# Last mixture's combine: rows read place by place behind a data-dependent gate, all adding on VectorE

## The reference, cut to what matters

```python
w, sel = _route(x, gate_weight, expert_bias)          # 4 distinct experts of 16 per token
cw = (one_hot(sel, NUM_EXPERTS) * w[..., None]).sum(1)
def body(acc, inp):
    g, u, d, we = inp
    y = silu(x @ g.T) * (x @ u.T) @ d.T
    return (acc + we[:, None] * y, None)
out, _ = lax.scan(body, zeros_like(x), (gate_proj, up_proj, down_proj, cw.T))
...
x = x + tanh(g_ffn[3]) * (out + shared)
```

## Time and profile before

| | us |
|---|---|
| median of 3 runs | 1233.58 |
| the profiled execution's own time | 1233.05 |
| its span, first to last instruction | 1231.3 |
| last tile's scatter starts on POOL | 1194.59 |
| first read of the combine issued | 1197.97 |
| DVE's 64 additions | 1201.25 to 1227.69 |

### The profile page before, as it was taken

The page is one execution under the profiler, slowest core; times in us unless marked ns, Lnnn a source line. Parts: engine busy times, 40 slices in busy tenths (PEclk is TensorE's granted clock), DMA queues, the critical chain, the costliest instruction groups (busy, mean ns, idle before and its releaser), DMA issues. The chain is left out here.

```text
span 1231.3 us, 25490 instructions
## 1 busy us (share of the span) xinstructions
PE 1056.1 (86%) x7158; PEld 776.4 (63%) x7159; DVE 747.1 (61%) x2777; ACT 497.3 (40%) x1341; POOL 605.1 (49%) x945
## 2 busy tenths in 40 slices
PE   4988799999999998699998989948886958799970
PEld 4556688886777775356556778725554536588850
DVE  6766545234444443789975565566778776555548
ACT  0056321213333332378772234415664633244430
POOL 5652006762333334666662535535655766455550
PEclk9988799999999998699998999957999978899995
DMA  9889922223333333422520245340001622466648
GB/s 399 243 321 399 405 111 85 103 95 88 108 104 108 108 104 114 139 95 87 215 70 28 80 136 154 118 146 1 2 2 49 242 80 98 129 165 163 165 123 325
DMA packets 71646, 175.75 MB, mean 143 GB/s; under 512 B 11438, under 2 KB 38318, under 8 KB 70446
## 3 DMA queue, kind: packets, MB, share of 16 engines
q1 hardware_dynamic: 50297, 117.84, 29.3%
q0 software_dynamic: 17664, 48.91, 10.9%
q10 hardware_dynamic: 3600, 7.95, 1.7%
HBM read 85.89 MB, written 88.76 MB: 142 GB/s over the span
## 5 line engine op out<-in xcount | busy, mean ns | idle before, releaser
L2349 PE MATMUL bank<-weights,xT 128*128 x832 | 240.6, 412 | 0.2 <-ACT xT L2445 0.2
L2168 POOL DMA_INDIRECT slots_out<-weights,y_rows x128 | 122.7, 959 | 114.5 <-DVE y_rows L2616 67.1
L2162 POOL DMA_INDIRECT slots_in<-xn_wide,row_in x110 | 106.7, 970 | 118.2 <-ACT rows L2421 58.7
L2349 PEld LDWEIGHTS bank<-weights,xT 128*128 128x128 f32 x832 | 142.4, 191 | 24.6 <-issue 0.7
L2168 POOL DMA_INDIRECT slots_out<-pack,y_rows x80 | 76.7, 959 | 137.0 <-DVE y_rows L2616 112.4
L2445 ACT COPY xT<-bank 128x256 f32<-128x256 f32 x208 | 77.5, 373 | 115.1 <-PE bank L2341 114.9
L2258 PE MATMUL bank<-xT,weights 128*128 128x256 f32 x416 | 105.1, 398 | 2.3 <-ACT xT L2409 2.3
L1574 PE MATMUL bank<-ctx,weights 32*128 32x256 f32 x512 | 77.8, 449 | 31.0 <-DVE weights L1730 25.3
L1647 ACT ACTIVATE weights<-bank 128x512 f32<-128x512 f32 x128 | 72.6, 596 | 57.9 <-PE bank L1582 57.9
L1730 DVE TENSOR_REDUCE weights<-bank 128x2 f32<-128x512 f32 x128 | 85.6, 682 | 15.3 <-PE bank L1574 15.0
L2593 DVE TENSOR_TENSOR weights<-weights,bank 128x128 f32<-128x128 f32 x128 | 36.8, 288 | 93.3 <-ACT weights L2449 93.2
(11 more groups left out here) (436 smaller groups left out, 2435.4 us busy)
## 6 DMA issues: line engine op xcount, KB each, us to landing
slots_in<-gbias SPq DMA_DIRECT2D x11, 3072.0 KB, 25.6
weights<-slots_in SPq DMA_DIRECT2D x96, 132.0 KB, 2.3
xs_wide<-slots_in SPq DMA_DIRECT2D x72, 132.0 KB, 2.2
weights<-slots_out SPq DMA_DIRECT2D x17, 512.0 KB, 9.6
rows<-slots_out SPq DMA_DIRECT2D x16, 512.0 KB, 3.5
weights<-in_l_gu SPq DMA_DIRECT2D x1, 7040.0 KB
pack<-slots_in SPq DMA_DIRECT2D x40, 132.0 KB, 2.1
weights<-in_l_gu SPq DMA_DIRECT2D x1, 4352.0 KB, 13.7
```

Source lines behind the costliest of these rows:

```text
L2162: pool.indirect_dma_start(out=slots_in, in_=xn_wide[:, t, :], in_offset=None, out_offset=bass.IndirectOffsetOnAxis(ap=row_in[:, t, i:i + 1 ...
L2168: pool.indirect_dma_start(out=slots_out, in_=y[:, n % U, :], in_offset=None, out_offset=bass.IndirectOffsetOnAxis(ap=y_rows[:, n % U:n % U ...
L2349: last = nc.tensor.matmul(out, xT[:, n.c % 2, c, :], flat(gu_w[:, ds(e, 1), c, :]), start=(c == 0), stop=(c == C - 1 and layer != 2))
```

## The change

`combine_last()` goes. Its work moves to the end of the queues inside `mixture(3, ...)`:

- DVE works out in `rank_experts`, for the experts 12, 13, 14 and 15, how many turns of 8 tiles the tiles up to that expert take, times 16, into `turns_past` (four more small instructions).
- SP, when it has issued the last tile's load, does four times, for the places 3, 2, 1, 0: it reads a number of `turns_past` into a register, waits until all eight `stored[u]` have reached it, and issues the read. Places 3, 2 and 1 are one DMA of 2 MB each, into `ctx`, `ctxT` and `xn`, which nothing needs any more; place 0 is four DMAs of 512 KB (4 blocks each) into the space of the first 8 experts' weights. All pieces are now 1 KB.
- DVE goes from the loop straight into the same 64 additions, in pairs of blocks, places 3, 2, 1, 0 within a pair. An addition of place 3, 2 or 1 waits for that place's whole DMA, one of place 0 for the quarter that its block is in.
- The output stores are issued by SP, behind the reads.

The diff also has code for PE, ACT and POOL to take a part of the adding. It is not used: `TURNED` and `POOLED` are empty.

```diff
@@ rank_experts
+        if layer == 3:
+            turns = routed // 8
+            begun = rt["go_on"][:, 0:4 * turns].rearrange("p (e j) -> p e j", j=turns)
+            need = rt["go_on"][:, 4 * turns:4 * turns + 4]
+            step(nc.vector.tensor_scalar(need, cum[:, NE - 4:NE], 1.0 / 8, None, ALU.mult))
+            step(nc.vector.tensor_tensor(begun, need.unsqueeze(2).broadcast_to([P, 4, turns]),
+                                         numbers[:, 0:turns].unsqueeze(1).broadcast_to([P, 4, turns]), ALU.is_gt))
+            step(nc.vector.tensor_reduce(need, begun, AX.X, ALU.add))
+            step(nc.vector.tensor_scalar(turns_past[:], need, 16.0, None, ALU.mult))
+            yield
@@ mixture
+            if layer == 3:
+                row_home = (weights[:, 0:NB * D].rearrange("p (t d) -> p t d", t=NB), xn,
+                            ctxT[:].rearrange("p t c q -> p t (c q)"), ctx[:])
+                of_token = slots_out[0:NB * P * 4].rearrange("(t p i) d -> p t i d", p=P, i=4)
...
+                OWN = tuple(("rows", t, t + 1) for t in range(0, NB, 2))
+                TURNED, POOLED = (), ()
+                STORES = tuple((t, t + 2) for t in range(0, NB, 2))
...
+                def wait_row(eng, t, i):
+                    if i:
+                        eng.wait_ge(early_in[i], 16)
+                    else:
+                        eng.wait_ge(last_in[t // 4], 16)
@@ sync
+                if layer == 3:
+                    for i in (3, 2, 1, 0):
+                        past = sp.value_load(turns_past[0:1, 3 - i:4 - i], min_val=32, max_val=16 * (total // U))
+                        for u in range(U):
+                            sp.wait_ge(stored[u], past)
+                        if i:
+                            sp.dma_start(row_home[i], of_token[:, :, i, :]).then_inc(early_in[i], 16)
+                        else:
+                            for q in range(4):
+                                few = slice(4 * q, 4 * q + 4)
+                                sp.dma_start(row_home[0][:, few], of_token[:, few, 0, :]).then_inc(last_in[q], 16)
+                    for t0_, t1_ in STORES:
...
+                            sp.wait_ge(added, finished[t1_ - 1])
+                        sp.dma_start(io["out"][:, t0_:t1_, :], x[:, t0_:t1_, :]).then_inc(out_stored, 16)
+                    for u in range(U):
+                        sp.wait_ge(stored[u], total // U * 16)
+                    sp.wait_ge(out_stored, 16 * len(STORES))
@@ vector
-                for i in range(U):
-                    dve.wait_ge(stored[i], total // U * 16)
+                if layer < 3:
+                    for i in range(U):
+                        dve.wait_ge(stored[i], total // U * 16)
+                    return
...
+                    for i in (3, 2, 1, 0):
+                        for t in of:
+                            wait_row(dve, t, i)
+                            if i < 3:
+                                dve.wait_ge(added, done + 1 - len(of))
+                            nc.vector.scalar_tensor_tensor(x[:, t, :], row_home[i][:, t, :], weight[:, t, i:i + 1],
                                                            x[:, t, :], ALU.mult, ALU.add).then_inc(added, 1)
+                            done += 1
@@ the block that goes
-    def combine_last():
...
-                for t in range(NB):
-                    sp.dma_start(rows[:, t], of_token[:, t]).then_inc(ready[t], 16)
...
-                for t in range(0, NB, 2):
-                    act.wait_ge(added, place(t + 1, n - 1))
-                    act.dma_start(io["out"][:, t:t + 2, :], x[:, t:t + 2, :]).then_inc(out_stored, 16)
...
-                for pair in range(0, NB, 2):
-                    for i in range(n):
-                        for t in (pair, pair + 1):
```

More of the change, by code:

```diff
@@ L170, in _build @@
     tile_block = sb("tile_block", [1, ROUTED], I32)
+    turns_past = sb("turns_past", [P, 4], I32)
     lanes = sb("lanes", [P, 4])
@@ L2082, in mixture @@
                 gb = gbias[:].rearrange("p (e n) -> p e n", e=NE)
+            if layer == 3:
+                row_home = (weights[:, 0:NB * D].rearrange("p (t d) -> p t d", t=NB), xn,
+                            ctxT[:].rearrange("p t c q -> p t (c q)"), ctx[:])
+                of_token = slots_out[0:NB * P * 4].rearrange("(t p i) d -> p t i d", p=P, i=4)
+                last_in = [sem(f"last_in{i}") for i in range(4)]
+                early_in = [None] + [sem(f"early_in{i}") for i in range(1, 4)]
+                added, diag_ready, mixed, scaled, pooled = (
+                    sem(n) for n in ("added", "diag", "mixed", "scaled", "pooled"))
+                diag = row_space[:, 0:8 * P].rearrange("p (u i q) -> p u i q", u=2, i=4)
+                turned_banks = [bank[i] for i in (0, 1, 2, 3, 6, 7)]
+                OWN = tuple(("rows", t, t + 1) for t in range(0, NB, 2))
+                TURNED, POOLED = (), ()
+                STORES = tuple((t, t + 2) for t in range(0, NB, 2))
+                finished, done = {}, 0
+                for kind, *of in OWN:
+                    done += 4 * len(of) if kind == "rows" else len(of)
+                    for at, t in enumerate(of):
+                        finished[t] = done - (len(of) - 1 - at)
+                def wait_row(eng, t, i):
[3 more added lines that the diff above has]
+                        eng.wait_ge(last_in[t // 4], 16)
             E_I = m["E_I"]
@@ L2170, in _ @@
                                             ).then_inc(stored[n % U], 16)
+                if layer == 3 and POOLED:
+                    pool.wait_ge(sh_added, NB)
+                    for at, t in enumerate(POOLED):
+                        for i in (3, 2, 1, 0):
+                            pool.wait_ge(scaled, 4 * at + 4 - i)
+                            if i < 3:
+                                pool.wait_ge(pooled, 4 * at + 3 - i)
+                            nc.gpsimd.tensor_tensor(x[:, t, :], x[:, t, :], row_home[i][:, t, :], ALU.add
+                                                    ).then_inc(pooled, 1)
             @block.sync
@@ L2381, in _ @@
                 each_step(pe, step)
+                if layer == 3:
+                    for q, t in enumerate(TURNED):
+                        for i in (3, 2, 1, 0):
+                            wait_row(pe, t, i)
+                            pe.wait_ge(diag_ready, 4 * q + 4 - i)
+                            last = nc.tensor.matmul(turned_banks[q][:, 0:D], diag[:, q % 2, i, :], row_home[i][:, t, :],
+                                                    start=(i == 3), stop=(i == 0))
+                        last.then_inc(mixed, 1)
             @block.scalar
@@ L2460, in _, with weigh_ident, weigh @@
                 each_step(act, step)
+                def weigh_ident(q):
+                    if q >= 2:
+                        act.wait_ge(mixed, q - 1)
+                    for i in (3, 2, 1, 0):
+                        nc.scalar.activation(diag[:, q % 2, i, :], ident[:], ACT.Copy,
+                                             scale=weight[:, TURNED[q], i:i + 1]).then_inc(diag_ready, 1)
+                def weigh(t):
+                    for i in (3, 2, 1, 0):
+                        wait_row(act, t, i)
+                        nc.scalar.activation(row_home[i][:, t, :], row_home[i][:, t, :], ACT.Copy,
+                                             scale=weight[:, t, i:i + 1]).then_inc(scaled, 1)
+                if layer == 3 and TURNED:
+                    weigh_ident(0)
+                    weigh_ident(1)
+                    for at in range(3):
+                        weigh(POOLED[at])
+                        weigh_ident(2 + at)
+                    weigh_ident(5)
             @block.vector
@@ L2623, in _ @@
                 each_step(dve, tile_step)
-                for i in range(U):
-                    dve.wait_ge(stored[i], total // U * 16)
-    def combine_last():
[L2629 to L2640, removed]
-                for t in range(NB):
-                    sp.dma_start(rows[:, t], of_token[:, t]).then_inc(ready[t], 16)
-            @block.scalar
-            def _(act):
-                for t in range(0, NB, 2):
-                    act.wait_ge(added, place(t + 1, n - 1))
-                    act.dma_start(io["out"][:, t:t + 2, :], x[:, t:t + 2, :]).then_inc(out_stored, 16)
-                act.wait_ge(out_stored, 16 * NB // 2)
-            @block.vector
-            def _(dve):
-                for pair in range(0, NB, 2):
-                    for i in range(n):
-                        for t in (pair, pair + 1):
[L2656 to L2660, removed]
@@ new lines, in _ @@
+                if layer < 3:
+                    for i in range(U):
+                        dve.wait_ge(stored[i], total // U * 16)
+                    return
+                done = 0
+                for kind, *of in OWN:
+                    if kind == "bank":
+                        for t in of:
```

(11 more changed lines are left out.)

4 lines of the change are left out of this document (3 added, 1 removed).

## The result

The changed kernel takes 1235.59 us (median of 18 runs), the kernel before 1232.24 us in 18 runs beside it: ratio 1.0028, 95% interval 1.0020 to 1.0036. It is slower by 3.4 us, clear of zero and just under the 0.3% that the prediction took as its bound. The forecast was 1239.0 with a range of 1235.3 to 1245.1; the profiled execution's span is 1234.9 us (1231.3 before).

A forecast was written before the change was run, and what follows sets the result against it. The end was taken as DVE-bound with DMA close behind: gate 1184.9 + start-up 1.96 + pieces 20.2 + scatters 2.9 = 1209.96, plus 23.1 of additions to 1233.1, 5.4 us later; 1239.0 us on the median, range 1235.3 to 1245.1.

The forecast's parts named there:

- Gate: Before the reads: all four gates open together with tile 71 at 1184.9, reads starting 13.1 us earlier than at 1197.97.
- The first pair: Start of the additions: place 0 needs three 2 MB reads and a quarter of the fourth; only 6 additions fit before.
- 416 pieces an engine: Reads up to place 0's first quarter: 1 KB pieces at 48.5 ns, 20.2 us (17.1 to 26.2 by the bounds).
- eight scatters: Scatters of tiles 72 to 79 on the same DMA engines during the reads: 0.366 us each, 2.9 us.
- start-up: Fixed time from a read's issue to its landing, beside the pieces' transfer: 1.96 us.
- 58 additions: DVE's remaining additions after place 0's first quarter lands: 57 x 0.397 + 0.48 = 23.1 us, without further waits.
- The 2 KB row: Profile row of 2 KB reads of the same tensor and strides: 89.8 ns each, half of it 44.9 ns.
- the half and the straight line: Two prices for a 1 KB piece: half the 2 KB price, 44.9 ns; line through 4 KB and 2 KB, 52.2 ns.
- the page's rule: Packet overhead of about 3 cycles beside one per 32 bytes: 44.1 ns a 1 KB piece, read time 18.3 us.
- the trace disagrees: Remark that 2 KB pieces at 372 GB/s contradict the page's 207 GB/s at 512 KB row pitch, within the 0.2 expensive-pieces rival.
- Hidden edits: Routing instructions, block change, two waits per addition and stores on SP, costed at nothing; worst cases 1.0 and 4.0 us.
- small pieces cost nearly nothing: Rival on the reads: 41.2 to 44.4 ns a piece, loss 2.4 to 3.7 us, 1236.0 to 1237.3; chance 0.31.

The follow-up runs named there:

- x1: Changed kernel with SP issuing the reads by quarters of the blocks, 16 DMAs of 512 KB, each addition waiting for its own quarter and place; ratio to before 0.9919.
- x2: Changed kernel with only DVE's order turned: all 16 blocks of place 3, then of places 2, 1, 0; ratio to the kernel before 0.9930.
- x5: Changed kernel without the scatters of tiles 72 to 79, run twice; ratios to the kernel before 0.9992 and 1.0015.
- x4: Changed kernel with all four gates at 160, when all 80 tiles have landed; ratio to the kernel before 1.0107.
- x8: Changed kernel with early-gate reads by blocks in 4 KB pieces and four of 16 blocks added up by PE; ratio to the kernel before 0.9902.

## Why the prediction was right in its steps and too high in its size

- **Gate.** All four gates were to open together with tile 71, 2.4 us after its scatter's start. Measured 2.48; the read of place 3 was issued at 1184.60 (1184.9 forecast), the next two right behind it. Right, by the count of tiles from the data. Between the first three issues SP's register load and waits took 1.1 and 0.9 us (the bound was 1 us for each), hidden beside the transfers.
- **The first pair.** That 6 additions fit in ahead of place 0 and 58 follow is what the trace shows, and x1 and x2 show it as the cause: with either order turned, 11.3 to 12.4 us go.
- **Reads.** First issue to place 0: forecast 25.1 us, measured 23.57. Its parts:

| term, us | forecast | measured |
|---|---|---|
| 416 pieces an engine | 20.2 (48.5 ns) | 19.1 (45.9 ns, from place 2 to place 1) |
| eight scatters | 2.9 | 2.2 (x5), 1.7 (x4) |
| start-up | 1.96 | by difference 2.2 (x5: 21.32 - 19.1), 2.8 (x4: 21.91 - 19.1) |
| 58 additions | 23.1 | 23.0 (1208.17 to 1231.21) |

  The two mis-sized terms are the price of a piece, 1.1 us too high, and that of the scatters, 0.7 to 1.2 us too high. Both prices came from shares of the DMA view, and when the engines are full the share counts some time more than once: the line below says 110.4% for 2079 packets in 6 us, which would be 51 ns a packet, whereas 351 GB/s say 46.7 ns. The 2 KB row had 101.9%: 89.8 ns by the share, 88.1 by its 372 GB/s. But this explains little of the piece's price. With 88.1 alone put right, the middle of the half and the straight line is 46.9 ns; with the 4 KB price by bytes too (158.3 ns, from the 414 GB/s of x8) the half is 44.1, the line 53.0 and the middle 48.5 again. What was off is the choice of the middle: 45.9 ns lies near half of the 2 KB price. Why the scatters cost less than their share is not settled. By bytes, 1 MB at 364 GB/s, they come to 2.9 us as well; one possible reason is that the engines of the changed kernel are not full before about 1187, so that the first of the eight, tile 72's of 1183.75, could move beside the reads at no cost.

The DMA view of the changed kernel, window 1206:1212:

```profile
DMA packets 2079, 2.10 MB, mean 351 GB/s; under 512 B 64, under 2 KB 2040, under 8 KB 2079
q1 hardware_dynamic: 2079, 2.10, 110.4%
```

- **By the page's rule** (the Trainium skill, DMA: Bandwidth & Descriptors, Why small descriptors are slow), an estimate from that page scaled from the 4 KB row, a piece would have cost 44.1 ns; the trace has 45.9, closer to the rule than to my 48.5. Scaled from the 158.3 ns of x8 the rule gives 42.3. The warning in the same page's section Latency and other measured facts is for the distance from one partition's row to the next. Here that is 4 KB, and the 512 KB lie between blocks within one partition, so neither nor this run tests it; "the trace disagrees" in the prediction said too much. What the trace shows is that 1 KB of every 4 KB came at 351 to 364 GB/s.
- **Hidden edits.** The routing instructions and two waits per addition cost nothing that the trace shows: the pace of the additions is 0.396 us from one start to the next, and so it was before (63 in 25.04 us). The last store took 2.0 us and the tail after DVE's end 3.7 us (3.6 before), both as forecast.
- **The sum.** DVE ended at 1231.21, 3.5 us later than before where 5.4 were forecast; counted from tile 71's scatter it is 3.9, and the 1.5 us between are those of the reads above. The price of a piece was within the forecast's 44.4 to 52 ns, but with the cheaper scatters the loss of the medians, 3.4 us, landed in the band that I had given to "small pieces cost nearly nothing" (2.4 to 3.7 us). The chance of 0.65 for slower by over 0.3% went to a case that came out at 0.28%. Of the 3.4 us from the forecast 1239.0 to the measured 1235.59, 1.3 us are no term of the sum at all: the kernel before has a median of 1232.24 us in 18 runs, where the sum started from 1233.58 in 3.

That a gate of its own for each place would pay with other routings, where the four turns differ, wasn't tried.

## What to carry to other kernels

When a transfer is split another way, compare the order in which its parts land with the order in which the consumer wants them: here the 10.5 us that an earlier start gave were spent, and 3.9 more, because the first pair of additions needed the last of four reads. Start the transfer early, land in the order of use, and only then count pieces. A gate that depends on data is worth counting on the data: the four gates were one.

## What the runs showed that I had not expected

- SP is held when several reads are queued: the first two reads of 2 MB took 0.40 and 0.88 us to issue, but the third took 6.02 and one of the last four 5.99, as long as a whole 2 MB takes to move (5.88). Whatever stands behind them on SP waits. In the changed kernel nothing did; in x1 SP issued its last read at 1200.96, so that the first store went out at 1202.81, 10.9 us after its pair was done, which cost nothing since only the last store stands at the end.
- While the reads ran, scatters took a median of 5.8 us from issue to landing instead of 2.4; no addition waited for them.

In the changed kernel, the lines of the two reads and of the scatters, the latter in the window 1183:1212:

```profile
L2247 SPq DMA_DIRECT2D xn_wide<-slots_out x1: 6017/6017/6017, 1187.8 to 1187.8; - x1
L2251 SPq DMA_DIRECT2D weights<-slots_out x4: 1421/1427/5991, 1194.8 to 1203.7; - x4
slots_out<-weights,y_rows POOLq DMA_INDIRECT x9, 5.8
```
